# Pairwise-interaction tower on one core: burst weights in a ring of 16 places, deeper one-hot and product rings, and a new order of all work

## The reference

```python
e = jnp.stack([tbl_0[ids[:, 0]], ..., tbl_39[ids[:, 39]]], axis=1)   # 2048 x 40 x 32
z = einsum('bke,kef,bkf->bk', e[:, I], W, e[:, J])                  # 780 pairs (I < J)
h = jnp.concatenate([z, dense_ctx], axis=1)                         # 796 columns
h = jnp.maximum(h @ W_top1 + b_top1, 0.0)                           # 512
h = jnp.maximum(h @ W_top2 + b_top2, 0.0)                           # 256
y = h @ W_top3
```

## Time and profile before

| | |
|---|---|
| time, median of 3 runs | 1132.43 us (1129.46 to 1133.22) |
| profiled execution, span from first to last instruction | 1130.1 us |
| busy: PE, DVE, ACT, POOL | 875.4, 540.3, 327.1, 412.3 us |
| mean granted TensorE clock | 0.814 of full |
| DMA traffic | 39.24 MB, mean 35 GB/s |

### The profile page before, as it was taken

One profiled execution on the slowest core, in us unless ns is written; L12 is line 12 of the kernel. 1 busy time (PEld: TensorE's weight loads), 2 busy tenths in 40 slices (PEclk: granted clock), 3 DMA queues, 4 the chain that ended last, 5 costly groups with the idle time before them and its releaser, 6 DMA issues.

```text
span 1130.1 us, 16792 instructions
## 1 busy us (share of the span) xinstructions
PE 875.4 (77%) x7232; PEld 201.8 (18%) x7232; DVE 540.3 (48%) x510; ACT 327.1 (29%) x243; POOL 412.3 (36%) x436
## 2 busy tenths in 40 slices
PE   4322358788779995886895789779889787899998
PEld 1000012121112220121121112112112111122223
DVE  3100067364345660452380447337245264688884
ACT  4001047553246380032260134127244000000002
POOL 6777341533353137324517151451624604000000
PEclk8555598887578895886796788989779788899999
DMA  4100044201001020100101002010010102011010
GB/s 155 32 14 13 12 145 127 63 7 52 9 11 53 12 72 13 44 16 18 38 22 41 5 10 75 9 47 4 12 34 8 39 3 58 8 39 29 1 36 3
DMA packets 30489, 39.24 MB, mean 35 GB/s; under 512 B 11376, under 2 KB 19200, under 8 KB 30160
## 3 DMA queue, kind: packets, MB, share of 16 engines
q1 hardware_dynamic: 14880, 25.59, 7.7%
q0 software_dynamic: 13824, 7.11, 4.3%
q10 hardware_dynamic: 1712, 5.48, 1.4%
HBM read 21.93 MB, written 0.07 MB: 19 GB/s over the span
## 4 chain that ended last, share of the span: by engine, by line
PE 65%; another core or an unknown queue 17%; issue 11%; DVE 3%; ACT 2%; SPq 1%; DMA 1%; DVEq 0%; ACTq 0%
PE t_ps L857 27%; PE z_ps L881 18%; PE x_ps L898 10%; PE x_ps L806 7%; PE x_ps L911 2%; SPq L543 1%; DVE prod L727 1%; ACT one_hot L602 1%; PE t_ps L911 1%; DVE one_hot L689 1%; PE t_ps L898 1%; PE t_ps L829 0%; DVE z_sb L673 0%; ACT one_hot L605 0%
## 5 line engine op out<-in xcount | busy, mean ns | idle before, releaser
L727 DVE TENSOR_TENSOR prod<-t_ps,e_t 128x1024 f32<-128x1024 f32 x392 | 459.4, 1213 | 425.2 <-remote 300.6
L558 POOL DMA_INDIRECT rows<-cold_tables,idx x432 | 412.1, 954 | 550.1 <-DVE e_t L734 420.2
L857 PE MATMUL t_ps<-e_t,w_sb 32*64 32x512 f32 x3120 | 362.0, 658 | 73.8 <-issue 53.6
L881 PE MATMUL z_ps<-prod,select 128*32 128x512 f32 x1560 | 243.5, 639 | 21.7 <-issue 21.0
L602 ACT ACTIVATE one_hot<-hot_sb,row_number 128x2048 bf16<-128x2048 f16 (+1 forms) x75 | 140.6, 1875 | 110.3 <-remote 87.4
L898 PE MATMUL x_ps<-z_sb,w_sb 128*32 128x512 f32 x704 | 131.1, 635 | 24.4 <-issue 22.5
L605 ACT ACTIVATE one_hot<-one_hot 128x2048 bf16<-128x2048 bf16 (+1 forms) x75 | 134.3, 1791 | 2.4
L857 PEld LDWEIGHTS t_ps<-e_t,w_sb 32*64 32x64 f32 x3120 | 74.6, 136 | 323.0 <-issue 221.6
L806 PE MATMUL x_ps<-one_hot,tables 128*32 128x512 bf16 x1194 | 97.8, 402 | 27.3 <-issue 22.6
L806 PE MATMUL t_ps<-one_hot,tables 128*32 128x512 bf16 x198 | 45.3, 501 | 92.1 <-issue 87.9
L689 DVE TENSOR_SCALAR one_hot<-hot_sb,row_number 128x2048 bf16<-128x2048 f16 (+1 forms) x47 | 33.9, 744 | 133.2 <-remote 130.0
(11 more groups left out here) (33 smaller groups left out, 98.6 us busy)
## 6 DMA issues: line engine op xcount, KB each, us to landing
e_t<-e_t SPq DMA_DIRECT2D x64, 128.0 KB
e_t<-e_t SPq DMA_DIRECT2D x112, 64.0 KB
rows<-cold_tables,idx POOLq DMA_INDIRECT x432
hot_sb<-hot_ids SPq DMA_DIRECT2D x11, 512.0 KB, 3.6
w_sb<-w_lay ACTq DMA_DIRECT2D x1, 1792.0 KB, 7.0
z_sb<-hot_tables SPq DMA_DIRECT2D x4, 320.0 KB, 5.1
w_sb<-w_lay ACTq DMA_DIRECT2D x1, 1216.0 KB
w_sb<-w_lay ACTq DMA_DIRECT2D x1, 896.0 KB, 4.6
```

The costliest lines, as they stand in the source:

```text
L558: pool.indirect_dma_start(out=rows[:, slot, span, :], out_offset=None, in_=table, in_offset=bass.IndirectOffsetOnAxis(ap=idx[:, n, span:sp ...
L727: nc.vector.tensor_tensor(prod[:, u % PROD_SLOTS, 0:banks, :], t_ps[:, at:at + banks, :], by, ALU.mult).then_inc(mult_done, 1)
L857: mm = nc.tensor.matmul(t_ps[cols, at + n, :], w_sb[part, b, cols], e_t[part, e_slot(k, of[side]), :], start=True, stop=True)
L881: mm = nc.tensor.matmul(z_ps[E * q:E * q + E, :], select[:, E - PER - PER * s:2 * E - PER - PER * s], prod[:, (u + q // 2) % PROD_SLOTS, q ...
```

## The change

Three sizes change and the order is written anew. The one-hot ring gets 6 places for 4, the product ring 8 units for 6. To make room `w_sb` keeps 16 bursts' weights in place of 50: a ring of 4 pieces of 4 bursts. A quarter is 13 pieces (the last of two bursts), so 52 loads replace 4. ScalarE issues three of the first four and SP all others; ahead of burst b (a multiple of 4) it waits until every unit before b is generated, and then loads the piece three ahead, into the place of the piece just finished. TensorE waits at each piece's first burst for its load. Matmuls, products, gathers and copies are the same in number and shape; how one-hots are shared out changes by two (VectorE 47 to 45, ScalarE 75 to 77).

```diff
-HOT_SLOTS = 4
+HOT_SLOTS = 6
...
-PROD_SLOTS = 6
+PROD_SLOTS = 8
...
-W_PIECES = [(0, 4), (4, 6), (6, 8), (8, 10)]
+W_PIECE = 4
+W_RING = 4
+W_PIECES = -(-len(BURSTS) // W_PIECE)
...
 ORDER = """
-pippppipphpoohoOppoohopphpohOppohpoophphpopohhhooOhpoohpohhopohphhpotopOhhohhhpgpoophhhphOhrhoohhoooppghhhOooh
...
+ppppppppppippppoooOpihoohoppohOhpphphhhohhohopophooohhhhOppOppoohpoOhpphhohohopohoOoohhghopohhhOorohOhpgohoOhh
...
-        w_sb = sb("w_sb", [P, len(BURSTS), P])
+        w_sb = sb("w_sb", [P, W_RING * W_PIECE, P])
...
+        def w_piece(k, b):
+            return k * W_PIECES + b // W_PIECE
+
+        def w_slot(k, b):
+            return w_piece(k, b) % W_RING * W_PIECE + b % W_PIECE
+
         def load_w(engine, n):
-            a, b = (begin_of(c) for c in W_PIECES[n])
-            engine.dma_start(w_sb[:, a:b, :], w_lay[:, a:b, :]).then_inc(w_loaded[n], 16)
+            k, piece = divmod(n, W_PIECES)
+            a, b = piece * W_PIECE, min(piece * W_PIECE + W_PIECE, len(BURSTS))
+            slot = w_slot(k, a)
+            engine.dma_start(w_sb[:, slot:slot + b - a, :], w_lay[:, a:b, :]).then_inc(w_loaded[n % W_RING], 16)
...
-                elif kind == "gen" and BURSTS[step[2]][0] == 0 and BURSTS[step[2]][1] % 2:
+                if kind == "gen" and step[2] % W_PIECE == 0:
+                    ahead = w_piece(k, step[2]) + W_RING - 1
+                    if W_RING <= ahead < chunks * W_PIECES:
+                        sp.wait_ge(gen_done, first_unit(k, step[2]))
+                        load_w(sp, ahead)
+                if kind == "gen" and BURSTS[step[2]][0] == 0 and BURSTS[step[2]][1] % 2:
...
-                if k == 0:
-                    for n, (first, _) in enumerate(W_PIECES):
-                        if b == begin_of(first):
-                            pe.wait_ge(w_loaded[n], 16)
+                if b % W_PIECE == 0:
+                    n = w_piece(k, b)
+                    pe.wait_ge(w_loaded[n % W_RING], 16 * (n // W_RING + 1))
```

More of the change, by code:

```diff
@@ L51 @@
 BURSTS.insert(SMALL_LAYER, (-1, -1))
-BEGIN = [BURSTS.index((0, c)) if c else 0 for c in range(GROUPS)]
 UNITS = 2 * len(BURSTS)
 T_SLOTS = 3
-PROD_SLOTS = 6
+PROD_SLOTS = 8
 BATCHES = len(BURSTS) - 1
@@ L91 @@
 FOLD_RING = 5
-W_PIECES = [(0, 4), (4, 6), (6, 8), (8, 10)]
-def begin_of(c):
-    return BEGIN[c] if c < GROUPS else len(BURSTS)
+W_PIECE = 4
+W_RING = 4
+W_PIECES = -(-len(BURSTS) // W_PIECE)
 def first_unit(k, b):
@@ L164 @@
 ORDER = """
-pippppipphpoohoOppoohopphpohOppohpoophphpopohhhooOhpoohpohhopohphhpotopOhhohhhpgpoophhhphOhrhoohhoooppghhhOooh
[L166 to L172, removed]
+ppppppppppippppoooOpihoohoppohOhpphphhhohhohopophooohhhhOppOppoohpoOhpphhohohopohoOoohhghopohhhOorohOhpgohoOhh
+oghhhhrogrhghOhgrtrOghOrgOhorghrgOthhgrrgrOgrghOhgtrhgOOrOrgrghhOghgOrgtrrgrhgOOrhOghhgOorrghrghhgorrgOrhgOhtr
+grrghOOOhgrgrhtgrrOOghhgrOghrgorrghOrOghhgrgrhgorrgOrhgOhrgrhgrgO1t1Ogor1g1rg1O1gtrrOgr1g1rg11gOtrrg11grrghhgO
+OrhOOghtrgrrghhhgOrhgrhgrOhgrOO1grOrg11g1rtg1r1grhOgrhgrohhghOrOghhgrorgrthghrhg11gr1Ogrrg11Ogr1grrg2oorOg222g
+2otrgrrrgr2tg22grhghrghrghhgrOrOOgrhghrhg1rg1rOtg1rg1rg1O1grrg1t1gr1gor1gOrrg11grrgrOhOOghtOOhhOghrgrhrghhgrhg
+hrOg1O1gr1g1rOg1t1grrrg33OrroghhgrOhghrgrhthgrrgOrhghrOghOhg1rg1rtg11g11grrrgrrg22gr2tgr2gr2gr2g22g3rgrrg3rgr1
+grgrg11g1rtg11grrg11gt1rgrrgr1g11grrg1rg1rg1rtgrrg1rg11grrg11g1t1g1rg1rgrrg2rg2rgrrgr2gr2g2rg2rg22tg1rg1rtgrrg
+r1g1rg11g11g1rg1rg1rg1rgr1gr1grg1rg1rg3rgrrg3rg11rr1111112222222233
 """
@@ L338, in tower_kernel @@
         selects_loaded = sem("selects_loaded")
-        w_loaded = [sem(f"w_loaded{n}") for n in range(len(W_PIECES))]
+        w_loaded = [sem(f"w_loaded{n}") for n in range(W_RING)]
         consts = sem("consts")
@@ L611, in _ @@
                     nc.scalar.copy(e_t[:, e_slot(k, c), :], bank_of(use)).then_inc(x_taken, 1)
-                    if k == 0 and c + 2 < len(W_PIECES):
+                    if k == 0 and c + 2 < W_RING:
                         load_w(act, c + 2)
-                    elif k == 0 and c == len(W_PIECES) - 2:
+                    elif k == 0 and c == W_RING - 2:
                         act.dma_start(w1_sb[:, :, :], w1_lay).then_inc(consts, 16)
@@ L856, in gen @@
                             cols = slice(P // 2 * side, P // 2 * side + P // 2)
-                            mm = nc.tensor.matmul(t_ps[cols, at + n, :], w_sb[part, b, cols],
+                            mm = nc.tensor.matmul(t_ps[cols, at + n, :], w_sb[part, w_slot(k, b), cols],
                                                   e_t[part, e_slot(k, of[side]), :], start=True, stop=True)
```

## The result

The changed kernel takes 1140.98 us (median of 11 runs, 1132.62 to 1148.54) and the kernel before 1133.34 us (11 runs, 1126.3 to 1141.17) on the same chip: a ratio of 1.0072, 95% interval 1.0036 to 1.0108. It is slower by about 0.7%, beyond the 1140 us of the range. The profiled span is 1139.1 us against 1130.1.

The account below looks back on a forecast made before the run. TensorE's work and the gathers together were taken to bound the kernel, neither count altered. Terms -5.4 + 3 + 0 + 1 + 2.6 - 2.6 = -1.4 put the span at 1129, forecast 1130 us, range 1119 to 1140.

Parts of the forecast that it names:

- Start of the first quarter: Up to the later first turn, behind 41 lookups and 6 gens: ScalarE's work just fits, 0 us, from -2 to +6.
- Its rival: Between the eleventh lookup and the first turn, ScalarE's one-hots make TensorE stand 5 to 6 us: 1136 to 1138; chance 0.14.
- No pairs of items: Two pairs of touching items come apart, as the smallest spacing of turns is 7.7 us: -5.4 us.
- the fourth rival: Pairs stay, because turns (1,9) and (2,3) touch and others slip together: 1133 to 1135; no chance of its own.
- half of it: If the two turns spaced 7.7 us touch, half of the 5.4 us saving is kept.
- What runs under the gathers: Under each item's gathers about 160 records pass; the work that fits falls from 128 to 124.5 us: +3 us.
- the prediction's own sign: The prediction is wrong if the loss per item outside the first quarter moves by more than 0.3 us.
- Deeper rings: More places for one-hots and products ease the first quarter's items and the waits for products: -2.6 us.
- the waits for VectorE: Between gathers, where few other steps separate bursts, TensorE waits for products: 6 us before, 9 now, +2.6.
- SMALL: Waits for transfers between burst 40's red and SMALL, over four quarters: 2.4 us saved, 3.4 lost, +1.
- Weight ring: 48 more loads of 256 KB at most, each issued at least 24 us ahead of need: hidden, cost 0.
- Instruction fetch: By the rule of mostly hidden fetching, gathers would cost TensorE nothing, sum 1130; the 0.7 us steps decided against it.

Follow-up runs that it names:

- the cut kernels: The kernel before and the changed kernel, each gathering only the first six items: 749.94 us (0.6628) and 748.86 us (0.6613 of the kernel before).
- pair_apart: Changed kernel with turn (1,9) four letters earlier and (2,3) six later: 1145.47 us, 1.0052 of the kernel before; changed kernel on that chip 1151.67 us.
- turns_on_reds: Changed kernel with 12 turns outside the first quarter moved so that counted work under the gathers rises: 1140.74 us, 0.9981 of the kernel before.
- ring_only: Kernel before with only the weight ring and its 48 loads added, old order, old one-hot and product rings: 1142.97 us, 1.0012.
- no_reload: Changed kernel without the 48 later weight loads and TensorE's waits for them: 1151.28 us, 1.0077 of the kernel before.

## Why the prediction was wrong

**The bound was read rightly.** TensorE is short of instructions while GpSimd gathers: without the later gathers 381 us go, and with pauses 338.

**Start of the first quarter, "0, from -2 to +6": it cost 5.0.** This is the first step that failed. Its rival (chance 0.14) had the place, the engine and the size, but its sign did not come as it stood: "It decides if ScalarE is busy without gaps from 140 us to the first turn". ScalarE had gaps of 0.27, 1.83 and 3.95 us and was busy without gaps only from 161; the five DMA issues in its program (4.4 us) were not counted, and the working compared sums of 33 and 30 us where two late one-hots decide, 5.2 us together. I had also excused it with "the same count on the order before, to its second turn, has ScalarE as close". That was true, and the cut kernels show it, but there an item's gathers lay over the wait.

**"No pairs of items", -5.4: not reached.** The spacing of 7.7 touched, as the fourth rival had it. `pair_apart` shows what that alone costs, some 0.4%, 4.6 to 5.5 us, more than the 2.7 of the "half of it" set against it.

**"What runs under the gathers", +3: the sign held, the working did not.** Together with the pairs the prediction had -2.4 for the items, and the 14 items outside the first quarter came out 5.9 dearer, 8 us off: the second step that failed. Two orders counted 15 us apart were 4 us apart, so the record count is no measure of an item's cost. The term's own count does not stand either: the expectation of `turns_on_reds` has 143 us for the changed kernel where the prediction has 124.5, and counting 160 records from each of the 21 turns (32 for a gen, 24 for a lookup, 16 for a red or a layer step) gives 140.6 before and 139.8 now. How many records pass did not change: a mean of 166 matmuls and loads in 21.7 us for single items behind the first quarter, in either kernel. By the prediction's own sign, 0.3 us per item, the move from 17.7 to 18.3 says that it is wrong. Why singles cost 18.3 in place of 17.7 is open; that turns moved in either direction took the loss back (on another chip, and the pair was gone in both) shows only that their placement bears on it.

**Deeper rings, -2.6 and net 0 with the waits for VectorE: right in kind, too small.** With the old order they gained 0.55%, 6 us; the first quarter's items fell from 125.0 us lost (`ring_only`) to 119.3.

**SMALL, +1: the mechanism was right.** TensorE was to stand some 3 us ahead of the last SMALL, for transfers; it stood 3.21:

```profile
1111.92 1.84 PE L838 MATMUL t_ps<-z_sb,w_sb 32*64 32x512 f32 x16 [3.21 <-DMA z_sb<-z_sb]
```

**Weight ring, 0: right.** `ring_only` is 0.12% from before, inside its interval, and `no_reload` gains nothing. The Trainium skill (DMA: Bandwidth & Descriptors, "Issuing engines are not separate DMA queues") has the DMAs of SP, ACT and POOL interleave on the same 16 DMA engines, and by that rule gathers would have lengthened. They did not: with 9.8 MB more a gather still goes out every 1.25 us (GpSimd 15.09 to 15.16 us busy for 16 of them), as before.

**Instruction fetch.** The Trainium skill (Runtime: NRT & Kernel Launch, "Instruction fetch mechanics") has fetching mostly hidden. By that rule the gathers would cost nothing, and the windows above are against it where GpSimd issues more than four gathers without a gap. But they do not show that the fetch is what is late, and the kernel before speaks against it. The page counts 57 packets on queue q8, of 16 KB, for TensorE's 14464 records, about one for every 254. From 60 to 120 us, inside the long run of gathers, that queue moved a single packet, and TensorE's matmuls came one by one, 2.8 us apart:

```profile
q8 instruction: 1, 0.02, 0.1%
...
61.67 0.59 PE L806 MATMUL t_ps<-one_hot,tables 128*32 128x512 bf16 x1 [2.21 <-issue]
64.48 0.58 PE L806 MATMUL t_ps<-one_hot,tables 128*32 128x512 bf16 x1 [2.22 <-issue]
67.27 0.59 PE L806 MATMUL t_ps<-one_hot,tables 128*32 128x512 bf16 x1 [2.21 <-issue]
```

A late packet would make TensorE stand once for each packet, not at each instruction. "Issue" says that no semaphore was outstanding; what holds each instruction back while GpSimd issues is open.

## What to carry to other kernels

When an engine's idle time reads "issue" while another engine issues DMAs back to back, first break up the burst: a few lines gained 30% where a new order of the whole kernel moved 1%. Counting a stretch by sums hides the one late instruction at the head of a queue; walk the queue, DMA issues included, up to the step that releases the next engine. A wait is free only as long as something slower lies over it, and reordering can pull the two apart.

## What was not expected of the hardware

A pause of 1.6 us after four gathers keeps TensorE near its full rate, and with one after five the kernel takes some 110 us more than that. The slowdown sets in with the fifth gather issued in a row (19 to 22 matmul records for each of the first four gathers, then 9, 5, 4 and 3). The median of the unchanged kernel was between 1130.5 and 1142.6 us from chip to chip, more than the whole change, so only ratios on one chip can be read.
